# Two of 25 gathered neighbour rows of a step's second and fourth tile replaced by selection products on TensorE

## What is computed

```python
# layer 0, per batch
h = maximum(layernorm(x), 0)
vals, idx = top_k(where(A != 0, -arange(N), -inf), 25)   # the 25 first neighbours of each node
feats = h[idx]                                           # 25 rows of 256 per node; missing ones -inf
agg = feats.max(axis=2)                                  # and maximum with 0 where degree <= 25
x = x + relu(concat([h, agg]) @ W0 + b0)
# layer 1, per batch
h = maximum(layernorm(x), 0)
hidden = h @ W1.T
attn = leaky_relu(attn1[:, None] + attn2[None, :], 0.2)
attn = softmax(where(A > 0, attn, attn - 1e12))
x = x + attn @ hidden + bias
```

## Time and profile before

| | |
|---|---|
| median of 3 runs | 4229.43 us (4226.17 to 4229.52) |
| the profiled execution | 4228.84 us, its span 4226.7 us |
| POOL busy | 3064.6 us (73%), 3200 gathers |
| DVE busy | 2596.7 us (61%) |
| PE busy | 2441.5 us (58%) |
| ACT busy | 1565.1 us (37%) |
| DMA | 867.56 MB, mean 205 GB/s |
| mean granted TensorE clock | 0.756 of full |

### The profile page before, as it was taken

How to read it: one execution, slowest core, us unless ns; L and a number is a source line. 1 busy time by engine, 2 the same in 40 slices (tenths; PEclk the granted TensorE clock), 3 DMA queues, 4 the chain that set the end, 5 groups by cost and what they waited for, 6 DMA issues and landing times. The chain is left out here.

```text
span 4226.7 us, 34008 instructions
## 1 busy us (share of the span) xinstructions
PE 2441.5 (58%) x8788; PEld 1510.5 (36%) x8788; DVE 2596.7 (61%) x6764; ACT 1565.1 (37%) x1748; POOL 3064.6 (73%) x3204
## 2 busy tenths in 40 slices
PE   1213345656555656565666565566556566656898
PEld 0111123433333434333334333343333343434565
DVE  5654566666666666666665676566676666566653
ACT  3112233334343434343434433334433334434354
POOL 4777777777777777777777777777777777777740
PEclk6555567777777878777878777777777777777899
DMA  7455568777777777777777777777777776777530
GB/s 288 150 189 174 189 180 232 195 219 214 230 211 228 204 223 216 217 220 219 212 215 216 216 228 211 228 207 209 218 228 215 224 207 213 214 211 223 179 106 35
DMA packets 477367, 867.56 MB, mean 205 GB/s; under 512 B 308298, under 2 KB 309204, under 8 KB 456660
## 3 DMA queue, kind: packets, MB, share of 16 engines
q0 software_dynamic: 153600, 419.64, 36.0%
q1 hardware_dynamic: 305140, 378.64, 28.8%
q10 hardware_dynamic: 18432, 67.12, 4.2%
HBM read 690.98 MB, written 119.54 MB: 192 GB/s over the span
## 5 line engine op out<-in xcount | busy, mean ns | idle before, releaser
L560 POOL DMA_INDIRECT near<-table_dram,idx x3200 | 3064.4, 958 | 1011.4 <-issue 961.1
L1406 PE MATMUL acc<-hid,wgt 128*128 128x257 f32 x4096 | 1051.5, 404 | 61.6 <-ACT wgt L642 54.4
L964 DVE TENSOR_TENSOR highest<-near,highest 128x512 f32<-128x512 f32 x1280 | 890.4, 696 | 43.8
L1406 PEld LDWEIGHTS acc<-hid,wgt 128*128 128x128 f32 x4096 | 817.0, 203 | 199.1 <-ACT wgt L642 72.2
L961 DVE TENSOR_TENSOR highest<-near 128x512 f32<-128x512 f32 x128 | 89.7, 701 | 814.8 <-DMA near<-table_dram,idx 813.4
L606 ACT ACTIVATE nm_t<-adj_i,big_c 128x2048 bf16<-128x2048 int32 x128 | 501.5, 3944 | 7.0 <-DMA adj_i<-in_adj_dram 3.4
L636 ACT ACTIVATE pen<-a_b,a_rise 128x512 f32<-128x512 f32 x432 | 296.5, 690 | 427.0 <-DMA nm_c<-nm_q 397.9
L1339 PE MATMUL bank<-w_sb,h_t 128*128 128x256 f32 x1024 | 348.0, 499 | 134.4 <-ACT h_t L739 134.4
L642 ACT ACTIVATE wgt<-pen,a_slope 128x512 f32<-128x512 f32 x448 | 304.2, 679 | 292.4 <-PE pen L1399 254.6
L739 ACT ACTIVATE h_t<-bank 128x512 f32<-128x512 f32 x128 | 76.0, 594 | 849.3 <-PE bank L1331 849.3
L898 DVE MAX8 top<-key 128x8 f32<-128x256 f32 (+1 forms) x1024 | 351.4, 384 | 5.6
(11 more groups left out here) (161 smaller groups left out, 2355.4 us busy)
## 6 DMA issues: line engine op xcount, KB each, us to landing
adj_i<-in_adj_dram SPq DMA_DIRECT2D x128, 1024.0 KB
nmask_dram<-nm_t ACTq DMA_DIRECT2D x128, 512.0 KB
nm_q<-nmask_dram SPq DMA_DIRECT2D x28, 2048.0 KB, 8.7
near<-table_dram,idx POOLq DMA_INDIRECT x3200
h_q<-table_dram SPq DMA_DIRECT2D x32, 512.0 KB, 3.9
x_q<-in_x_dram SPq DMA_DIRECT2D x32, 512.0 KB, 5.4
xmid_dram<-x_q SPq DMA_DIRECT2D x32, 512.0 KB, 4.3
o_q<-xmid_dram SPq DMA_DIRECT2D x32, 512.0 KB, 8.0
```

Source lines behind the costliest of these rows:

```text
L560: pool.indirect_dma_start(out=near[:, t % 2, k, :], out_offset=None, in_=table, in_offset=bass.IndirectOffsetOnAxis(ap=idx[:, t, k:k + 1], ...
L964: nc.vector.tensor_tensor(highest[:, :], pair(k), highest[:, :], ALU.max).then_inc(mx_step, 1)
L1406: mm = nc.tensor.matmul(acc[:, t, 0:C + 1], wgt_part(j)[:, t * P:(t + 1) * P], hid[:, bass.ds(batch * NJ + j, 1), 0:C + 1].rearrange("p a ...
```

## The change

In steps 0 to 29 the tiles with t = 1 and t = 3 ("hot" tiles) gather 23 rows instead of 25. The last two are made on the chip, as a 0/1 matrix times the 2048 rows of the batch, which are held in SBUF:

- `tab` (128 x 16 x 256 f32) takes the place of h_q: SP loads the whole batch every fourth step (four loads of 512 KB), not one quad per step.
- ACT widens the two index columns of the tile to 128x2x128 (`hot_widened`); PE turns them with the identity into `highest` (`hot_turned_index`, two matmuls of 128 columns), ACT copies the result to `agg` and sets `highest` to zero (`hot_row_copy`).
- For each of 16 blocks k of 128 table rows DVE makes the two selection matrices of 128x128 by one comparison with a column of constants (`hot_rows_made`, 16 tensor_scalar of 128x256 f32 from SBUF to SBUF), in four buffers that lie in `bits` and `key2`; PE multiplies each by the block (`hot_products`, 2 matmuls of 128x128 with 128x256 f32) and accumulates both rows in `highest`. A mask waits until the product four before it is done.
- `maximum` of such a tile waits for the 16th product and then starts from `highest`; it has as many instructions as before.
- The ring of POOL's DMA descriptors is set to 8192 bytes (`dynamic_dma_scratch_size`), which makes room in SBUF.

```diff
+HOT_TILES = (1, 3)
+HOT = 2
+HOT_BUFS = 4
...
-        near = sb("near", [P, 2, S, C], F32)
+        near = sb("near", [P, 2 * S - HOT, C], F32)
+        tab = sb("tab", [P, NJ, C], F32)
...
-        h_q = sb("h_q", [P, T, C], F32)
...
+        hot_bufs = [flat[:, i * HOT * P:(i + 1) * HOT * P] for flat in (bits[:, :].bitcast(F32), key2[:, :, :].rearrange(
+            "p u g -> p (u g)")) for i in range(2)]
+        hot_idx_w = agg[:, :, :].rearrange("p u (i m) -> p u i m", i=HOT)
...
-                    sp.dma_start(h_q[:, :, :], table_quad(s % TRING)).then_inc(h_in, 16)
+                    if s % QB == 0:
+                        if s > 0:
+                            sp.wait_ge(table_out, 16 * s)
+                        for i in range(QB):
+                            sp.dma_start(tab[:, i * T:(i + 1) * T, :], table_quad((s + i) % TRING)).then_inc(h_in, 16)
...
-                    for k in range(S):
+                    for k in range(S - HOT if is_hot(s, t) else S):
...
+            def hot_widened(s, t):
+                act.wait_ge(idx_ready, 2 * s + t // 2 + 1)
+                nc.scalar.activation(hot_idx_w[:, t % 2, :, :], idx[:, t, S - HOT:S].unsqueeze(2).to_broadcast([P, HOT, P]), ACT.Copy
+                                     ).then_inc(hot_wide, 1)
...
+            def hot_row_copy(s, t):
+                n = hot_before(s, t)
+                act.wait_ge(hot_turned, n + 1)
+                nc.scalar.activation(agg[:, t % 2, :], highest[:, 0:HOT * P], ACT.Copy).then_inc(hot_rows, 1)
+                act.wait_ge(hot_rows, 2 * n + 1)
+                nc.scalar.activation(highest[:, :].rearrange("p (t m) -> p t m", t=T),
+                                     ident.unsqueeze(1).to_broadcast([P, T, P]), ACT.Copy, scale=0.0
+                                     ).then_inc(hot_rows, 1)
...
+            def hot_rows_made(s, t, groups=range(NJ // HOT_BUFS)):
+                n = hot_before(s, t)
+                for k in [HOT_BUFS * g + i for g in groups for i in range(HOT_BUFS)]:
+                    if k == 0:
+                        dve.wait_ge(hot_rows, 2 * n + 1)
+                    if k >= HOT_BUFS:
+                        dve.wait_ge(hot_used, NJ * n + k - HOT_BUFS + 1)
+                    col = C_HOT + s // QB % (TRING // QB) * NJ + k
+                    nc.vector.tensor_scalar(hot_bufs[k % HOT_BUFS], agg[:, t % 2, :], cst[:, col:col + 1], None, ALU.is_equal
+                                            ).then_inc(hot_made, 1)
...
             def maximum(s, t):
+                if is_hot(s, t):
+                    dve.wait_ge(hot_used, NJ * (hot_before(s, t) + 1))
...
             def attend_setup(a, lo):
-                largest(a2_row, nm_q, junk, range(T), as_n)
+                for t in range(T):
+                    largest(a2_row, nm_q, junk, (t,), as_n)
+                    hot_rows_made(a + LAG, 1, (t,))
...
                 if "index" in stages:
                     index_words(s + 1, 1)
+                if "gather" in stages:
+                    dve.wait_ge(b2_free, b2.n + 1)
+                    hot_rows_made(s, 3)
                 gathered(3)
...
+            def hot_products(s, t):
+                n = hot_before(s, t)
+                pe.wait_ge(hot_rows, 2 * n + 2)
+                for k in range(NJ):
+                    pe.wait_ge(hot_made, NJ * n + k + 1)
+                    for i in range(HOT):
+                        mm = nc.tensor.matmul(highest[:, i * C:(i + 1) * C], hot_bufs[k % HOT_BUFS][:, i * P:(i + 1) * P],
+                                              tab[:, k, :], start=False, stop=(k == NJ - 1), skip_group_check=True)
+                    mm.then_inc(hot_used, 1)
...
                 gathered(0)
+                if "gather" in stages:
+                    hot_products(s, 1)
                 if "attend" in stages:
                     attend_setup(a)
...
                     if "index" in stages and c == 3:
                         index_prep(s + 1, 1)
+                    if "gather" in stages and c == 3:
+                        hot_products(s, 3)
...
-    nc = _bacc.Bacc("TRN2", target_bir_lowering=False, num_devices=1)
+    nc = _bacc.Bacc("TRN2", target_bir_lowering=False, num_devices=1, dynamic_dma_scratch_size=8192)
```

More of the change, by code:

```diff
@@ L106, in shape_constants @@
         c[:, C_CODE + q] = BR * (q // QB % (TRING // QB)) + N + 0.25
+    for b in range(TRING // QB):
+        for k in range(NJ):
+            c[:, C_HOT + b * NJ + k] = BR * b + QR * (k // T) + T * np.arange(P) + k % T
     return c
@@ L328, in two_layers, with is_hot, hot_before, landed @@
         block = ctx.enter_context(nc.Block())
+        def is_hot(s, t):
+            return s < LAST - 1 and t in HOT_TILES
+        def hot_before(s, t):
+            return len(HOT_TILES) * min(s, LAST - 1) + (sum(u < t for u in HOT_TILES) if s < LAST - 1 else 0)
+        def landed(s, t):
+            tiles = [(r, u) for r in range(s + 1) for u in (t % 2, t % 2 + 2) if (r, u) <= (s, t)]
+            return sum(S - HOT if is_hot(r, u) else S for r, u in tiles)
         def schedule(step):
@@ L557, in step @@
                     pool.nop(nofuse=True)
-                    for k in range(S):
+                    for k in range(S - HOT if is_hot(s, t) else S):
                         attention(s, stages, t, k)
+                        spilt = t % 2 == 1 and k >= S - HOT
                         pool.indirect_dma_start(
-                            out=near[:, t % 2, k, :], out_offset=None, in_=table,
+                            out=tab[:, k - (S - HOT), :] if spilt else near[:, t % 2 * S + k, :], out_offset=None, in_=table,
                             in_offset=bass.IndirectOffsetOnAxis(ap=idx[:, t, k:k + 1], axis=0),
@@ L955, in index_rest @@
                 index_write(pair, ix_n)
-            def maximum(s, t):
-                dve.wait_ge(near_in[t % 2], 16 * S * (2 * s + t // 2 + 1))
-                pair = lambda k: near[:, t % 2, k:k + 2, :].rearrange("p a c -> p (a c)")
-                mx_n = Count()
-                nc.vector.tensor_tensor(highest[:, :], pair(0), pair(2), ALU.max).then_inc(mx_step, 1)
-                for k in range(4, S - 1, 2):
+            def hot_rows_made(s, t, groups=range(NJ // HOT_BUFS)):
+                if not is_hot(s, t):
+                    return
+                n = hot_before(s, t)
[7 more added lines that the diff above has]
+                                            ).then_inc(hot_made, 1)
@@ new lines, in maximum @@
+            def maximum(s, t):
+                dve.wait_ge(near_in[t % 2], 16 * landed(s, t))
+                rows = near[:, t % 2 * S:, :]
+                pairs = [rows[:, k:k + 2, :].rearrange("p a c -> p (a c)") for k in range(0, S - HOT - 1, 2)]
+                if is_hot(s, t):
+                    dve.wait_ge(hot_used, NJ * (hot_before(s, t) + 1))
+                elif t % 2 == 0:
+                    pairs.append(rows[:, S - HOT:S, :].rearrange("p a c -> p (a c)"))
+                else:
+                    pairs.append(tab[:, 0:HOT, :].rearrange("p a c -> p (a c)"))
+                mx_n = Count()
+                if is_hot(s, t):
+                    nc.vector.tensor_tensor(highest[:, :], pairs[0], highest[:, :], ALU.max).then_inc(mx_step, 1)
+                    others = pairs[1:]
+                else:
+                    nc.vector.tensor_tensor(highest[:, :], pairs[0], pairs[1], ALU.max).then_inc(mx_step, 1)
+                    others = pairs[2:]
+                for pair in others:
@@ L963, in maximum @@
                     dve.wait_ge(mx_step, mx_n.next())
-                    nc.vector.tensor_tensor(highest[:, :], pair(k), highest[:, :], ALU.max).then_inc(mx_step, 1)
+                    nc.vector.tensor_tensor(highest[:, :], pair, highest[:, :], ALU.max).then_inc(mx_step, 1)
                 dve.wait_ge(mx_step, mx_n.next())
-                nc.vector.tensor_tensor(agg[:, t % 2, :], near[:, t % 2, S - 1, :], highest[:, 0:C], ALU.max
+                nc.vector.tensor_tensor(agg[:, t % 2, :], rows[:, S - HOT - 1, :], highest[:, 0:C], ALU.max
@@ L1237, in step @@
                     attend_setup(a, lo)
+                elif "gather" in stages:
+                    hot_rows_made(s, 1)
                 finished(0)
```

52 lines of the change are left out of this document (39 added, 13 removed).

## The result

The changed kernel takes **4621.52 us** (median of 4 runs, 4616.96 to 4625.24), the kernel before 4227.8 us on the same chip: ratio 1.0932 with a 95% interval of 1.0913 to 1.0951. The forecast was 4626 us, 4400 to 4740.

The account below looks back on a forecast made before the run. POOL's gathers set the pace, with the DVE-ACT-PE ring nearly as long. That ring: 125.9 + 0.2 - 1.5 + 1.0 + 17.4 - 0.9 = 142.1 us; 4228.8 + 421 - 20 - 4 = 4626 us, range 4400 to 4740.

Parts of the forecast that it names:

- Two rings: POOL's gathers, 125.9 us per step, and the chain through DVE, ACT and PE, 120.9 without its 5.01 us wait.
- Removed gathers: On POOL, 4 gathers fewer per step at 1.25 us each take 5.0 us off POOL's ring.
- Second tile: Masks between DVE's four 128x2048 instructions add 5.2 us, replacing the wait for gathers; net +0.2 us per step.
- The clock gain of -1.5: PE's product before chunk 0 would run at the high clock, 1.99 instead of 3.52 us: -1.5 us per step.
- The small pieces: ACT's widening before chunk 0, 0.6 us, and PE's two index matmuls before the third tile's product, 0.4 to 0.5: +1.0.
- Products of the fourth tile: On PE between the index matmuls and chunk 4, uncovered: 2.2 + 15.2 = +17.4 us per step.
- Maximum of the fourth tile hidden: On DVE it slides by 15 us but stays hidden beside chunks 4 to 7, which take 18.9 us.
- the ring: Once per step through DVE, ACT and PE, from one end of the statistics to the next; forecast at 142.1 us.
- Given back: Masks for the later chunks have arrived by the time PE reaches them: -0.9 us per step.
- rival 2: Part hidden: waits for turned masks or the clock in chunks 2 and 3 absorb half of 17.4; about 4400, chance 0.13.
- The rule on the shared port: Masks on DVE hold up POOL's descriptor writing, 0.31 us each; POOL's ring 129.9 us, time 4349, chance 0.04.
- the four slower cases: Ring through PE, 4626, chance 0.65; part of cost hidden, 4400, 0.13; low-clock products, 5270, 0.06; POOL slowed by masks, 4349, 0.04.

Follow-up runs that it names:

- The run with the products behind: The changed kernel with the fourth tile's products placed behind chunk 7 on PE instead of ahead of chunk 4, same work: 4901.3 us, one run.
- masks alone: The kernel before, all 25 rows gathered, plus the 32 comparisons of 128x256 per step on DVE, results unused, no products: 4256.66 us, ratio 1.0066.

## Why the prediction was right

- **The bound.** Two rings of nearly equal length: POOL 125.9, the other 120.9 without its one wait for gathers. Shown: 121.3 with 4 gathers left out and 121.6 with 12.
- **Removed gathers**, 5.0 us of POOL: right as a price (135 us for 30 steps alone, against at most 150), and irrelevant for the sum.
- **Second tile**, +5.2 in place of the wait, net +0.2. Measured +5.4 at the residual, and chunk 0 starts at 51.9 against 51.8. The masks, an estimate of 0.3 us, took 0.353, inside its bounds.
- **The clock gain of -1.5** did not come. PE was at the high clock (granted 1.00) through the second tile's products, but then had short pauses again (2.72 us busy of the next 5.50), and the granted clock fell within the index matmuls that follow (2.87 us, where 1.96 is the high clock). The product ahead of chunk 0 took 3.78 us at 0.51 (3.52 before); over the 26 rounds 3.66 and 3.68.
- **The small pieces**, +1.0, cost nothing on the path. In the mean it is 5.6 us from the end of the index words to chunk 0 (before 5.8), and 6.8 us from the end of chunk 3 to the end of the index matmuls in both. Ahead of the third tile's product in the loop above PE waited 0.24 us for ACT behind the two index matmuls, where it waited 0.69 without them: they took the place of a wait. So chunk 3 ends at 83.3 us as before, where the sum, with 0.6 of the pieces counted by then, had it 0.7 earlier.
- **Products of the fourth tile**, 17.4: in the loop the gap was 1.98 (2.2 forecast), the products 14.1 (15.2). I took 0.475 us for a product, from a group of four with its start and end; in a longer row they come every 0.44. Over the 26 rounds chunk 4 starts 16.5 us later behind chunk 3, so the term was 0.9 us too large. This and the 1.0 of the small pieces nearly cancelled the missing clock gain.
- **Maximum of the fourth tile hidden**, yes: it ends at 115.5 in the ring, chunk 7 at 125.4. The run with the products behind shows what it costs uncovered.
- **Given back** 0.9: measured 0.6 in chunks 4 to 7 (19.6 to 19.0), of which 0.4 are shorter waits of PE; another 0.2 behind chunk 7. Chunks 0 to 3, where rival 2 saw slack, took 31.4 us before and after: their waits for masks moved along with the ring.
- **POOL** stood 17 us before row 12 where 20 were forecast, and 5 more, not named, before row 16 of the third tile, which waits for the second tile's maximum.
- **Sum:** 26 x 16.2 - 20 - 4 forecast, 26 x 15.6 - 9 - 0 measured by the ring. The savings of steps 0 to 3 were overstated: the gathers came 18 us earlier, but the ring's first round only 9. The ring was put 0.6 us per round too long, 16 us in all, and the savings 15 us too large; that both sums come to 397 us is luck, and so is part of the ring's own 142.1 against 141.5. The mechanism was right without it.
- **The rule on the shared port** ("SBUF — State Buffer", "Who interferes with whom", in the Trainium skill) lets the instruction that comes first hold the port for its whole length, so each comparison that began first would have held up POOL's descriptor writing. The trace does not agree: masks alone left gathers at 0.959 us in the mean, and those that began during a mask at 0.949. So here the contention is on DVE's side, and small. Whether these comparisons ran in the two-port mode of that rule, no run here shows.
- **The descriptor ring** was costed at nothing because POOL had room. That holds at 8192 bytes even where POOL has none, but the step to 4096 costs 170 us; the profile of before could not have told where between them it begins.
- **The chances:** those of the four slower cases add up to 0.88, not 0.87, and that of a faster kernel is 0.10.

The best version found is the change on the second tile alone, 4212 to 4213 us, 0.3 to 0.4% faster than the kernel before.

## What to carry to other kernels

An engine that issues without a pause is the bound only as far as the next ring allows: follow every other chain once round a step, and count the waits for the busy engine that lie on it, for their sum bounds what relieving this engine can bring. Here that was 5 us per step, and leaving out 12 gathers brought no more per step than leaving out 4. All of DVE's waits for gathers together would say too much: before the change it waited 2.4, 5.5, 11.2 and 3.6 us per round ahead of its four tiles, and only the second of these lies on the ring; leaving out 4 gathers brought 4.5 us per round, 12 of them 4.3. Work that is moved to an engine which is "58% busy" can cost its full length if it is put in that engine's order between two links of the ring, and nothing if it falls where the ring waits: added to the kernel before, equal products cost 0 us net in the second tile and 11.4 in the fourth, and 15.6 in the fourth once the second had used up the wait.

## What the hardware showed that I had not expected

- A smaller descriptor ring for POOL can cost time: in the kernel before 8192 bytes cost none (ratio 1.0001), 4096 bytes 4.0%. The gathers are not longer (0.956 us); the idle time before single ones is, up to 5.5 us, and the profile shows it as the engine's own issue.
- A f32 comparison of 128x256 from SBUF to SBUF takes 332 ns at least, a f32 product of 128x128 with 128x256 0.44 us in a row at the high clock.
- With more work on TensorE its mean granted clock was 0.845 in place of 0.756, and 0.811 with the same work behind chunk 7. Yet the stretches ahead of chunk 0 and at chunk 3 stayed at the low level (granted 0.51 and 0.50; 3.78 and 3.63 us for four products).
